# Graph network on one core: the equality one-hots of a group made by two wide VectorE instructions in place of six narrow ones

## The chip, the cores and the metric

The kernel runs on one core of a Trainium2 chip. The metric is the device time of one execution in microseconds (us). Before the change it is 1136.53 us, the median of 3 runs (1135.17 to 1138.17).

## The reference, cut to what matters

Two graph layers run over 3125 nodes with 128 features and 100000 edges, which are sorted by destination. The first layer takes, for each destination, the maximum over its edges of a message; the second takes means over the edges, twice.

```python
# layer 0
msgs = z[edge_dst] @ Wd + z[edge_src] @ Ws + edge_weight[:, None] * ww[None, :] + bm
agg = jax.ops.segment_max(msgs, edge_dst, num_segments=n)
x = layernorm(x + relu(z @ W1a + agg @ W1b + b1) @ W2 + b2)
# layer 1, twice: a mean over the edges' source rows, then dense layers
agg = jax.ops.segment_sum(x[src], dst, num_segments=n_nodes)
mean = agg / jnp.maximum(deg, 1.0)[:, None]
```

## The kernel before

The edges are worked off in 196 groups of 512 (the last has 160 real edges in one superbatch). A group has two superbatches of 256 edges, a superbatch two halves (`u`) of 128. A counter `k` steps through the groups; each engine has its own instruction order, written out by hand, and in step `k` the engines work on neighbouring groups. What matters here:

- **GpSimd** gathers the source rows of a group from memory by four indirect DMAs (`gathers`, L1037) of 128 rows each. The index of a row is read from `src_n` in SBUF. Seven groups of the 196 (`PICKED`: 17, 28, 37, 48, 60, 80, 93) aren't gathered, and five (`OWN`) take three gathers in place of four. The ring `gring` holds four groups: the gathers of group g wait until TensorE has transposed group g - 4 (`t_ps`).
- **TensorE** in step k adds the edge weights' part (L1614) and transposes the gathered rows (L1626) for group k; then, in `adjacent(k-2)`, it multiplies the one-hots of group k-2 into a count matrix (L1675, L1678) and picks the maxima of its segments (L1685), which raises `ae_ps` by one for each superbatch; `products(k-1)` transposes the scan's result (L1665). Between these stand tile work and pieces of the second layer (L1748, L1706), and for the picked groups products with other one-hots (L1785).
- **VectorE** in step k runs the scan of group k over 512 columns (`scan`, L1225, one operand of which lies in PSUM), `pick(k-1)` (L1217) and `one_hots(k-1)`, then tile work, and in the steps before a picked group makes that group's source one-hots (L1303).
- `one_hots(g)` makes, for each superbatch and half, `hot_l` (128 edges by 128 columns: which source row within its tile), `hot_d` (128 by 325) and, once a superbatch, `hot_x` (128 by 25). TensorE waits for `made` before it uses them. The buffers are rings of `HR` = 4 superbatches, so VectorE waits for `ae_ps` before it writes them again.
- After step 195 the second layer's rest follows: L1748, L1861, L1875 and L1910 on TensorE.

Of the kernel before, what the change touches and what calls it, by code (L numbers as in the profile page):

```python
# [4 lines left out]
P = 128  # L5
# [4 lines left out]
NT = -(-N // P)  # L10
LASTN = N - (NT - 1) * P
SB = 256
NS = -(-E // SB)
# [6 lines left out]
COLS = NT * W  # L20
AW = N + W
AWORDS = NT * AW // 2
HR = 4
# [109 lines left out]
def supers(g):  # L133
    return range(2 * g, min(2 * g + 2, NS))
# [6 lines left out]
def gnn_kernel(nc, x, src, dst, w, Wm, bm, W1, b1, W2, b2, W1lT, b1l, W1rT, W2lT, b2l, W2rT, out):  # L141
    f32, i32, bf16, f16, f32r = mybir.dt.float32, mybir.dt.int32, mybir.dt.bfloat16, mybir.dt.float16, mybir.dt.float32r
    ALU, ACT = mybir.AluOpType, mybir.ActivationFunctionType
# [17 lines left out]
    with ctx:  # L161
# [3 lines left out]
        def sem(name):  # L165
            return ctx.enter_context(nc.semaphore(name))
# [196 lines left out]
        made, picked, ae_ps, ae_sb = sem("made"), sem("picked"), sem("ae_ps"), sem("ae_sb")  # L363
# [738 lines left out]
        def _(dve):  # L1102
# [97 lines left out]

            def usual():
                def one_hots(g):
                    for s in supers(g):
                        if s >= HR:
                            dve.wait_ge(ae_ps, s - HR + 2)
                        r = s % HR
                        for u in range(2):
                            nc.vector.tensor_scalar(hot_l[:, r, u, :], i_key[:, 0:P], lo_n[:, u, s:s + 1], None, ALU.is_equal)  # L1208
                            nc.vector.tensor_scalar(hot_d[:, r, u, :], i_key[:, 0:COLS], key_n[:, u, s:s + 1], None, ALU.is_equal)  # L1209
                        nc.vector.tensor_scalar(hot_x[:, r, 0:NT], i_hi[:, 0:NT], key2_n[:, s:s + 1], None, ALU.is_equal).then_inc(made, 1)  # L1210

                def pick(g):
                    if g >= 2:
# [91 lines left out]
                for k in range(SLOTS):  # L1305
# [5 lines left out]
                    if slots(k, 1) is not None:  # L1311
                        pick(k - 1)
                        one_hots(k - 1)
# [682 lines left out]
```

## Time and profile before

| | |
|---|---|
| median of 3 runs | 1136.53 us |
| the profiled execution | 1136.4 us |
| its span, first to last instruction | 1134.6 us |
| PE busy | 997.1 us (88%) |
| VectorE (DVE) busy | 894.9 us (79%) |
| GpSimd (POOL) busy | 757.0 us (67%) |
| ScalarE (ACT) busy | 500.8 us (44%) |
| mean granted TensorE clock | 0.958 |

Busy shares are means over the whole program. GpSimd's "issue" is time in which the engine waited for nothing that the profile shows, between two of its instructions. The VectorE instructions overlap at their ends, so the recorded duration of one is longer than the step from its start to the next one's start.

### The profile page before, as it was taken

The numbers are of one execution on the slowest core, as the hardware profiler recorded it, in microseconds if no ns is written. First come the engines' busy times: TensorE is split into PE (matmuls) and PEld (weight loads), VectorE is DVE, ScalarE is ACT, GpSimd is POOL, SyncE is SP. The second block draws the span as 40 slices with busy tenths as digits, with TensorE's granted clock in tenths as the row PEclk, the third lists the DMA queues.
The fourth block names the chain that finished last, engine by engine and source line by source line (L and its number), as shares of the span: only waits on it lengthen the run. The fifth ranks groups of instructions, "written<-read, shape, count | busy, mean of one in ns | idle before, by whom it ended". The sixth has DMA issues, their size and how long they took to land.

```text
span 1134.6 us, 23462 instructions
## 1 busy us (share of the span) xinstructions
PE 997.1 (88%) x6407; PEld 735.8 (65%) x6449; DVE 894.9 (79%) x3127; ACT 500.8 (44%) x1434; POOL 757.0 (67%) x802
## 2 busy tenths in 40 slices
PE   4689999999997999978797879886889899899997
PEld 4367767767765777756665656565556577656776
DVE  6488999999886999897777778777788788746455
ACT  3256766666542656533333323333324233312664
POOL 6657777777777777777777777777777777200332
PEclk9789999999997999989898889999999999999999
DMA  8724344344344343334434334433344354446221
GB/s 210 214 61 94 92 98 109 94 99 114 89 97 106 91 119 97 91 85 127 110 87 93 90 97 129 105 91 89 87 132 110 106 150 97 117 134 177 83 58 42
DMA packets 123128, 121.14 MB, mean 107 GB/s; under 512 B 24307, under 2 KB 106392, under 8 KB 122989
## 3 DMA queue, kind: packets, MB, share of 16 engines
q1 hardware_dynamic: 95920, 69.21, 22.7%
q0 software_dynamic: 23968, 49.13, 18.0%
q10 hardware_dynamic: 3101, 1.21, 0.4%
q8 instruction: 54, 0.88, 0.3%
q14 instruction: 85, 0.70, 0.2%
HBM read 105.60 MB, written 13.88 MB: 105 GB/s over the span
## 4 chain that ended last, share of the span: by engine, by line
PE 36%; POOL 30%; issue 15%; DVE 12%; DMA 3%; SPq 2%; ACT 1%; ACTq 1%; DVEq 0%
POOL area L1037 30%; PE bank L1910 7%; PE bank L1748 5%; PE bank L1685 5%; PE bank L1675 3%; PE bank L1626 3%; PE bank L1785 3%; DVE area L1225 2%; DVE area L1209 2%; PE bank L1665 2%; PE bank L1875 2%; DVE area L1208 2%; PE bank L1614 2%; PE bank L1861 1%; PE bank L1706 1%
## 5 line engine op out<-in xcount | busy, mean ns | idle before, releaser
L1037 POOL DMA_INDIRECT area<-zs_d,area x729 | 705.4, 968 | 234.8 <-issue 219.3
L863 ACT CAST adj_w<-bank 128x325 f32 x391 | 176.2, 451 | 472.5 <-PE bank L1685 415.1
L1225 DVE TENSOR_TENSOR_SCAN area<-area,bank 128x512 f32<-128x512 bf16 x196 | 249.7, 1274 | 144.1 <-PE bank L1626 126.5
L1209 DVE TENSOR_SCALAR area<-area 128x325 bf16<-128x325 f16 x782 | 249.5, 319 | 0.0
L1685 PE MATMUL bank<-area 128*128 128x104 f32 x1564 | 234.0, 294 | 0.1
L1208 DVE TENSOR_SCALAR area<-area 128x128 bf16<-128x128 f16 x782 | 212.1, 271 | 0.0
L1685 PEld LDWEIGHTS bank<-area 128*128 128x128 f32 x1564 | 204.7, 204 | 11.3 <-ACT area L869 1.9
L1675 PE MATMUL bank<-area 128*128 128x325 bf16 x782 | 157.2, 316 | 22.0 <-DVE area L1210 15.8
L1626 PE MATMUL bank<-ident,area 128*128 128x128 f32 x734 | 123.1, 291 | 45.8 <-DMA area<-zs_d,area 45.4
L1626 PEld LDWEIGHTS bank<-ident,area 128*128 128x128 f32 x734 | 78.1, 142 | 91.1 <-DMA area<-zs_d,area 57.2
L1748 PE MATMUL bank<-adj_w,area 128*128 128x512 bf16 (+5 forms) x497 | 108.5, 357 | 24.6 <-DMA area<-parts_d 8.6
L1665 PE MATMUL bank<-ident,area 128*128 128x128 f32 x782 | 121.0, 278 | 0.0
L869 ACT COPY area<-bank 128x512 f32<-128x512 f32 x196 | 118.3, 604 | 4.7 <-issue 3.3
L909 ACT CAST hot_r<-adj_w 128x512 fp32r<-128x512 bf16 x175 | 98.0, 622 | 48.3 <-DVE adj_w L1303 47.5
L1058 POOL CAST counts<-adj_w 128x512 fp32r<-128x512 bf16 (+2 forms) x45 | 28.2, 631 | 124.1 <-DVE area L1357 74.7
L1785 PE MATMUL bank<-hot_r,zs_r 128*128 128x512 f32 (+1 forms) x350 | 99.7, 414 | 0.4 <-issue 0.3
L1210 DVE TENSOR_SCALAR area<-area 128x25 bf16<-128x25 bf16 x391 | 97.4, 249 | 0.0
L1665 PEld LDWEIGHTS bank<-ident,area 128*128 128x128 f32 x782 | 96.1, 151 | 0.3 <-issue 0.3
L1614 PE MATMUL bank<-area,ww 9*128 9x512 bf16 x189 | 74.4, 394 | 20.9 <-DMA area<-wp_d 20.8
L1675 PEld LDWEIGHTS bank<-area 128*128 128x128 bf16 x782 | 61.6, 100 | 45.9 <-DVE area L1210 22.9
L1748 PEld LDWEIGHTS bank<-adj_w,area 128*128 128x128 bf16 (+1 forms) x525 | 48.6, 98 | 64.3 <-issue 21.4
L1678 PE MATMUL bank<-area 128*128 128x25 bf16 x390 | 74.5, 191 | 0.0
(174 smaller groups left out, 1067.6 us busy)
## 6 DMA issues: line engine op xcount, KB each, us to landing
area<-mask_d SPq DMA_DIRECT2D x195, 128.0 KB
area<-zs_d,area POOLq DMA_INDIRECT x729
area<-zs_d SPq DMA_DIRECT2D x640, 0.5 KB
area<-parts_d SPq DMA_DIRECT2D x20, 384.0 KB, 7.6
area<-wp_d SPq DMA_DIRECT2D x195, 9.0 KB
zr_d<-area SPq DMA_DIRECT2D x24, 128.0 KB
area<-zr_d SPq DMA_DIRECT2D x6, 512.0 KB, 4.5
area<-scale_d SPq DMA_DIRECT2D x11, 256.0 KB, 4.3
```

Of the source, the lines that this page charges most:

```text
L863: nc.scalar.copy(adj[:, :, bass.ds(at, W)], A_BANK[s % 2][:, 0:COLS].rearrange("p (h w) -> p h w", w=W))
L869: nc.scalar.copy(St[:, 0:n], S_BANK[:, 0:n]).then_inc(st_sb, 1)
L1037: pool.indirect_dma_start(gring[:, g % GR * 4 + s % 2 * 2 + u, :], None, x if g < RAW else zs_d[0:N, :], bass.IndirectOffsetOnAxis(ap=firs ...
L1208: nc.vector.tensor_scalar(hot_l[:, r, u, :], i_key[:, 0:P], lo_n[:, u, s:s + 1], None, ALU.is_equal)
L1209: nc.vector.tensor_scalar(hot_d[:, r, u, :], i_key[:, 0:COLS], key_n[:, u, s:s + 1], None, ALU.is_equal)
L1225: nc.vector.tensor_tensor_scan(S[:, g % 2, 0:n], mask[:, g % MR, 0:n], (L_BANK if g in PICKED else T_BANK[g % 2])[:, 0:n], S[:, (g + 1) % ...
L1626: last = nc.tensor.matmul(o[:, b * P:(b + 1) * P], rows, ident[:, :], start=False, stop=b == n // P - 1, is_transpose=True)
L1665: last = nc.tensor.transpose(S_BANK[:, b * P:(b + 1) * P], S[:, g % 2, b * P:(b + 1) * P], ident[:, :])
L1675: last = nc.tensor.matmul(o[:, 0:COLS], hot_l[:, r, u, :], hot_d[:, r, u, :], start=u == 0, stop=u == 1 and s == 0)
L1685: last = nc.tensor.matmul(o[:, 384:384 + WIDE * W].rearrange("p (n w) -> p n w", w=W), St[:, b * P:(b + 1) * P], sel[:, g % 2, u, s % 2, : ...
L1748: last = nc.tensor.matmul(o[:, 0:b - a], row[0:k, i * F:(i + 1) * F], adj[0:k, h, a:b], start=start and i == 0, stop=stop and i == 2)
L1785: last = nc.tensor.matmul(L_BANK[:, :], part_of[0:n, h - SPLITS[at][1], :], hot_r[u % HOTS][0:n, :], start=h == 0 and part_of is zs_high[a ...
```

## The change

For a group, the four instructions that made `hot_l` (128 columns each, a compare of `i_key` with one number per partition) become one compare of two tensors on 512 columns: `i_key`, in fp16 and repeated over superbatch and half, against `lo_n`, in f32 and repeated over the columns. The two that made `hot_x` (25 columns each) become one compare of two tensors on 50 columns. The four of `hot_d` stay, now side by side. The group waits once for `ae_ps`, for the count that its second superbatch waited for before; `made` rises by two at the end in place of one at a time.

```diff
                 def one_hots(g):
-                    for s in supers(g):
-                        if s >= HR:
-                            dve.wait_ge(ae_ps, s - HR + 2)
-                        r = s % HR
+                    s, m = 2 * g, len(supers(g))
+                    r = s % HR
+                    if s >= HR:
+                        dve.wait_ge(ae_ps, min(s + m, NS) - HR + 1)
+                    low = lo_n[:, :, s:s + m].unsqueeze(3).broadcast_to([P, 2, m, P])
+                    count = i_key[:, 0:P].unsqueeze(1).unsqueeze(1).broadcast_to([P, 2, m, P])
+                    nc.vector.tensor_tensor(hot_l[:, r:r + m, :, :].rearrange("p s u e -> p u s e"), count, low, ALU.is_equal)
+                    for n in range(m):
                         for u in range(2):
-                            nc.vector.tensor_scalar(hot_l[:, r, u, :], i_key[:, 0:P], lo_n[:, u, s:s + 1], None, ALU.is_equal)
-                            nc.vector.tensor_scalar(hot_d[:, r, u, :], i_key[:, 0:COLS], key_n[:, u, s:s + 1], None, ALU.is_equal)
-                        nc.vector.tensor_scalar(hot_x[:, r, 0:NT], i_hi[:, 0:NT], key2_n[:, s:s + 1], None, ALU.is_equal).then_inc(made, 1)
+                            nc.vector.tensor_scalar(hot_d[:, r + n, u, :], i_key[:, 0:COLS], key_n[:, u, s + n:s + n + 1], None, ALU.is_equal)
+                    carried = key2_n[:, s:s + m].unsqueeze(2).broadcast_to([P, m, NT])
+                    tiles_at = i_hi[:, 0:NT].unsqueeze(1).broadcast_to([P, m, NT])
+                    nc.vector.tensor_tensor(hot_x[:, r:r + m, 0:NT], tiles_at, carried, ALU.is_equal).then_inc(made, m)
```

On VectorE one step of the loop stood like this before, from the scan (L1225) and the pick (L1217) to the next step's source one-hots (L1303); `area` is the tensor that all of these buffers are cut from:

```order
L1225 SCALAR_TENSOR_TENSOR area<-area,bank 128x512 [waits scanned,l_mask0,t_ps]
L1217 TENSOR_TENSOR area<-area 128x52 [waits ae_ps]
L1208 TENSOR_SCALAR area<-area 128x128 [waits ae_ps]
L1209 TENSOR_SCALAR area<-area 128x325
L1208 TENSOR_SCALAR area<-area 128x128
L1209 TENSOR_SCALAR area<-area 128x325
L1210 TENSOR_SCALAR area<-area 128x25
L1208 TENSOR_SCALAR area<-area 128x128 [waits ae_ps]
L1209 TENSOR_SCALAR area<-area 128x325
L1208 TENSOR_SCALAR area<-area 128x128
L1209 TENSOR_SCALAR area<-area 128x325
L1210 TENSOR_SCALAR area<-area 128x25
```

In the changed kernel the lines behind the edit have numbers that are 5 higher, and the same step of VectorE stands like this:

```order
L1230 SCALAR_TENSOR_TENSOR area<-area,bank 128x512 [waits scanned,l_mask0,t_ps]
L1222 TENSOR_TENSOR area<-area 128x52 [waits ae_ps]
L1209 TENSOR_TENSOR area<-area 128x2x2x128 [waits ae_ps]
L1212 TENSOR_SCALAR area<-area 128x325 x4
L1215 TENSOR_TENSOR area<-area 128x2x25
```

Ten instructions have become six. The 512-column compare has moved to the front, right behind the pick, and the second wait on `ae_ps` has moved ahead of the whole block. The instructions of the other engines stand as they did.

## Rows read from the trace of the kernel before

**Rows 1.** Busy time of the engines in three stretches, with clock and DMA
```profile
73.00:490.00 417.00, 391.19 (x2609) 292.81 (x2618) 378.57 (x1396) 245.41 (x686) 318.33 (x324) 0.98 0.40 99
...
805.00:973.00 168.00, 151.05 (x1055) 106.38 (x1066) 139.67 (x469) 54.52 (x187) 127.47 (x134) 0.98 0.44 115
973.00:1135.00 162.00, 151.60 (x767) 112.72 (x768) 89.87 (x276) 70.54 (x152) 28.26 (x46) 0.98 0.36 101
```

**Rows 2.** GpSimd's waits from 73 to 973 us: total, times, longest
```profile
POOL area L1037 <- issue: 211.5, 694, 0.3
```

**Rows 3.** The gathers by line, 73 to 490 and 490 to 973 us
```profile
L1037 POOL DMA_INDIRECT area<-zs_d,area x324 | 319.2, 985 | 98.7 <-issue 95.7 <-PE bank L1626 3.1
...
L1037 POOL DMA_INDIRECT area<-zs_d,area x384 | 366.3, 954 | 117.1 <-issue 115.8 <-PE bank L1626 1.2
```

**Rows 4.** Timeline: last gather and scan of groups 161 and 195
```profile
805.01 0.95 POOL L1037 DMA_INDIRECT area<-zs_d,area  x1 [0.31 <-issue]
...
809.52 1.28 DVE L1225 TENSOR_TENSOR_SCAN area<-area,bank 128x512 f32<-128x512 bf16 x1 [2.08 <-PE bank L1626]
...
972.14 0.95 POOL L1037 DMA_INDIRECT area<-zs_d,area  x1 [0.30 <-issue]
...
980.80 0.74 DVE L1225 TENSOR_TENSOR_SCAN area<-area,bank 128x256 f32<-128x256 bf16 x1
```

**Rows 5.** VectorE groups by shape: busy us, mean ns
```profile
L1208 DVE TENSOR_SCALAR area<-area 128x128 bf16<-128x128 f16 x782 | 212.1, 271 | 0.0
...
L1210 DVE TENSOR_SCALAR area<-area 128x25 bf16<-128x25 bf16 x391 | 97.4, 249 | 0.0
...
L1347 DVE TENSOR_TENSOR area<-area 128x512 f32<-128x512 f32 x6 | 4.2, 692 | 0.2
```

**Rows 6.** Timeline: a pick, the block of one-hots, what follows
```profile
977.85 0.20 DVE L1217 TENSOR_TENSOR area<-area 128x52 f32<-128x52 bf16 x1
977.97 0.25 DVE L1208 TENSOR_SCALAR area<-area 128x128 bf16<-128x128 f16 x1
...
979.24 0.25 DVE L1208 TENSOR_SCALAR area<-area 128x128 bf16<-128x128 f16 x1
979.40 0.30 DVE L1209 TENSOR_SCALAR area<-area 128x325 bf16<-128x325 f16 x1
979.62 0.23 DVE L1210 TENSOR_SCALAR area<-area 128x25 bf16<-128x25 bf16 x1
979.75 0.22 DVE L1284 CAST area<-area 128x128 bf16<-128x128 f32 x1
```

**Rows 7.** Timeline: gathers that start under long VectorE instructions
```profile
12.54 1.22 DVE L1134 TENSOR_TENSOR adj_w<-adj_w 128x1020 f32<-128x1020 f32 x1 [2.59 <-ACT adj_w L805]
12.88 1.70 POOL L1037 DMA_INDIRECT area<-in_x_dram,first_n  x1 [0.30 <-issue]
...
21.02 1.20 DVE L1164 TENSOR_TENSOR adj_w<-adj_w 128x1024 f32<-128x1024 f32 x1
...
21.61 1.43 POOL L1037 DMA_INDIRECT area<-in_x_dram,area  x1 [0.30 <-issue]
...
39.24 1.22 DVE L1225 TENSOR_TENSOR_SCAN area<-area,bank 128x512 f32<-128x512 bf16 x1 [4.98 <-issue]
39.31 0.94 POOL L1037 DMA_INDIRECT area<-zs_d,area  x1 [0.30 <-issue]
```

**Rows 8.** Timeline: first and last gather counted under a new compare
```profile
83.11 0.25 DVE L1208 TENSOR_SCALAR area<-area 128x128 bf16<-128x128 f16 x1
...
83.46 0.94 POOL L1037 DMA_INDIRECT area<-zs_d,area  x1 [0.31 <-issue]
...
964.16 0.25 DVE L1208 TENSOR_SCALAR area<-area 128x128 bf16<-128x128 f16 x1
...
964.49 0.94 POOL L1037 DMA_INDIRECT area<-zs_d,area  x1 [0.30 <-issue]
```

**Rows 9.** TensorE's waits for the one-hots: total, times, longest
```profile
PE bank L1675 <- DVE area L1210: 15.8, 19, 2.7
```

## The prediction

> **What bounds the kernel now.** I first read the busy time by stretches [rows 1]. From 73 to 490 us TensorE is busy 391 of 417 us and VectorE 379, and from 805 to 973 they have 151 and 140 of 168: three engines run side by side at high load, and a share of the span doesn't say which one sets the pace. GpSimd looks the least loaded (318 of 417). So I next read what GpSimd waits for. Between 73 and 973 us, 694 of its pauses have nothing that releases them, 211.5 us in all, none longer than 0.3 us [rows 2]. The gathers stand in an unbroken row: 0.94 us for one, 0.30 of issue behind it, 1.25 us from start to start. With 708 of them in that stretch [rows 3] this is 885 of the 900 us, and the rest is gathers that took longer than 0.94. The ring of four groups never stops them. **GpSimd's chain of gathers is therefore the bound from 73 to 973 us**, and what lengthens or shortens a gather moves its end one for one.
>
> Two more stretches belong to the end time. The first is the start up to 72 us. The other runs from the last gather to the end, where TensorE is busy 152 of 162 us [rows 1]: TensorE alone. Between them lies a small reserve. In group 161 the scan starts 3.6 us after its last gather ends (805.01 + 0.95 to 809.52), and TensorE had been waiting for that landing. In group 195 it starts 7.7 us after (973.09 to 980.80) [rows 4]. At the end, the consumers are some 4 us behind where the gathers would let them be.
>
> **The change on VectorE.** In a block of today the 128-column compare takes 0.16 us from its start to the next start, the 325-column one 0.22, the 25-column one 0.13; the block takes 1.78 us (977.97 to 979.75) [rows 6]. The recorded 271 and 249 ns [rows 5] overlap, so multiplying those would double the gain. Removed are 4 x 0.16 + 2 x 0.13 = 0.90 us. No row shows a 512-column compare of an fp16 with an f32 tensor; the nearest is L1347, two f32 tensors of 512 columns in SBUF, 692 ns [rows 5], of which some 0.08 overlap the next: 0.61 us. From below it could be like the 25-column compare of one tensor (0.13), from above 0.69. I take 0.61, since one input here is f32 too. The 50-column one is like the pick on 52 columns, 0.12 us from start to start (977.85 to 977.97) [rows 6]. Added: 0.73. VectorE gains 0.17 us a group, 33 us of work over 196 groups. After 73 us this is worth nothing by itself, since VectorE isn't the bound; the cover is GpSimd's chain. Before 72 us five groups pass and the gathers do wait for TensorE: about -1 us.
>
> **The moved wait.** The whole block now waits for the first superbatch's L1685 of the group before; earlier half of it ran ahead. Where that wait binds, the block ends up to 0.89 - 0.17 = 0.7 us later. Behind it on VectorE stand tile work and the next scan; TensorE's L1675 of the next step waits for it, which it does 19 times now for 15.8 us [rows 9]. From below the cost is 0, from above 19 x 0.7 = 13 us of TensorE's waiting, and that counts only where TensorE has used up its distance to the gathers. I take 0; the reserve below covers a few us.
>
> **The change on GpSimd.** This is where I look for the time. At 12.54 us VectorE starts a compare of two SBUF tensors, which lasts until 13.76. A gather that starts at 12.88 takes 1.70 us and ends at 14.58, 0.82 after the compare's end. The one at 21.02 ends at 22.22, and the gather from 21.61 ends at 23.04: again 0.82 later [rows 7]. A free gather takes 0.94. So about 0.12 us after its start a gather needs something that a VectorE instruction with two SBUF inputs holds, and it waits for that instruction's end. A gather under the scan, which reads one operand from PSUM, isn't held: 0.94 us at 39.31 [rows 7]. The 128-column compares of today hold it little: in 490 to 973 us, where hardly any other one-hots are made, the mean gather is 954 ns against 944 free, 10 ns each [rows 3], or 7 us over 708 gathers for all ten instructions of a block. Six of ten go: -4 us.
>
> The new compare holds it for long. I count its hold from 0.07 us after its start (it starts under the pick's end) to 0.69. A read hits that with chance 0.62 / 1.25 = 0.50 and then waits 0.31 us in the mean: 0.154 us a group, 29 us over the 190 blocks after 72 us. Because the phases may not be random, I also laid the compare at the place of each block's first L1208 in the trace and took every gather whose start plus 0.125 falls within: 88 gathers, 27.3 us together. The first is the gather at 83.46 under the block from 83.11, the last that at 964.49 under 964.16 [rows 8]. I take 27. From below it is 0 if no read falls in, from above 0.69 x 0.69 / 2.5 x 190 = 36 us.
>
> [...]
>
> **The sum.** Gathers +27 (the new compare) and -4 (the old ones), start -1, and 3 of the 4 us of reserve, since the consumers catch up while the gathers run slower. The result is +19, made against the profiled execution's own 1136.4 us, which is the median within 0.1 us: **1155.5 us**.
>
> **Rivals.**
> [...]
> - *The compare runs at twice the rate* (0.05), as fp16 against bf16 might: 0.41 us, hold 0.34, 0.34 x 0.34 / 2.5 x 190 = 9 us: 1140 us. Against it: `lo_n` is f32.
> - *Nothing is held* (0.10): the two-tensor compare with repeated operands leaves the gathers alone, and the freed 128-column compares give 4 us back, the start 1: 1131 us, the other side. It decides if the new holding is below 5 us, that is under 26 ns a group. For it: neither of the held gathers lies under a compare with an fp16 input or repeated operands. Against it: the hold itself, twice to 0.01 us [rows 7].
> - *Full holding and the late wait* (0.06): 36 us from random reads on the whole 0.69, nothing given back, and TensorE pays part of the moved wait where it works off its backlog: 1172 us or more.
> - The forecast itself has 0.69, with its own range of 1146 to 1168.
>
> **How the numbers follow.** A measurement here tells 0.3%, 3.4 us, from no change. Slower: the forecast 0.69, the full holding 0.06, half of the first rival 0.05 and 0.02 of the second: 0.82. Within: 0.05 and 0.03, 0.08. Faster: 0.10. The range goes from 1139 (the first rival's time) to 1170; outside are the faster case, the lowest part of the first rival and most of the highest.
>
> **What would show it.** The mean of L1037 rises from 985 and 954 ns in the two stretches by some 30 ns each, with far more gathers above 1.0 us; each held one ends 0.82 us after the end of the compare at L1209. The row of gathers still has no wait of its own after 73 us and ends near 995 rather than 973. L1209 shows x196 near 690 ns, L1215 near 190; VectorE's busy time falls by some 30 to 60 us. The stretch behind the last gather keeps its 162 us within 3. I am wrong if the gathers keep their 985 and 954 ns, or if the compare takes much less than 0.6 us, or if GpSimd begins to wait for TensorE.

## The result

The changed kernel takes 1147.79 us (median of 9 runs, 1141.48 to 1150.76), the kernel before 1137.52 us (9 runs, 1135.17 to 1144.4). The ratio, taken between the means of the runs, is 1.0077, with a 95% interval of 1.0051 to 1.0103: **slower by 8.8 us, where 19 were forecast** (the medians lie 10.3 apart). The profiled execution took 1144.2 us, 7.8 more than that of before.

The gathers of the changed kernel by line, 73 to 490 us and 490 to 984 us (count, busy us, mean ns, idle before), to be read beside [rows 3]:

```profile
L1037 POOL DMA_INDIRECT area<-zs_d,area x323 | 320.6, 992 | 98.9 <-issue 96.0 <-PE bank L1631 2.9
...
L1037 POOL DMA_INDIRECT area<-zs_d,area x387 | 377.3, 975 | 118.0 <-issue 117.4 <-PE bank L1631 0.6
```

The mean rose from 985 to 992 ns in the first stretch and from 954 to 975 in the second. GpSimd's pauses are still nearly all without a releaser, beside [rows 2]:

```profile
POOL area L1037 <- issue: 213.1, 699, 0.3
```

The end of the chain in the timeline of the changed kernel, the last two gathers and the last scan, to be read beside [rows 4]:

```profile
981.72 1.16 POOL L1037 DMA_INDIRECT area<-zs_d,area  x1 [0.30 <-issue]
983.18 0.94 POOL L1037 DMA_INDIRECT area<-zs_d,area  x1 [0.30 <-issue]
...
989.09 0.74 DVE L1230 TENSOR_TENSOR_SCAN area<-area,bank 128x256 f32<-128x256 bf16 x1
```

The last gather ends at 984.1 us in place of 973.1: 11 us later. The last scan follows 5.0 us after it and no longer 7.7, so some 3 us of the reserve are used. From the last scan to the end of the span it takes 153.2 us (153.8 before).

VectorE by shape (count, busy us, mean ns), beside [rows 5]:

```profile
L1230 DVE TENSOR_TENSOR_SCAN area<-area,bank 128x512 f32<-128x512 bf16 x195 | 249.2, 1278 | 188.0 <-PE bank L1631 166.3 <-PE bank L1622 10.0 <-issue 7.2
L1212 DVE TENSOR_SCALAR area<-area 128x325 bf16<-128x325 f16 x782 | 190.1, 307 | 0.0
L1209 DVE TENSOR_TENSOR area<-area 128x512 bf16<-128x512 f16 x195 | 133.9, 687 | 11.6 <-PE bank L1690 11.3
...
L1215 DVE TENSOR_TENSOR area<-area 128x50 bf16<-128x50 bf16 x195 | 38.7, 198 | 0.0
```

The wide compare takes 687 ns. VectorE's busy time fell from 894.9 to 846.6 us, and what it saved turned into waiting: the scan now sits idle for TensorE's transposes for 166.3 us, and those wait for gathers. Two held gathers in the timeline of the changed kernel:

```profile
539.86 0.69 DVE L1209 TENSOR_TENSOR area<-area 128x512 bf16<-128x512 f16 x1
539.87 1.50 POOL L1037 DMA_INDIRECT area<-zs_d,area  x1 [0.30 <-issue]
...
655.01 0.68 DVE L1209 TENSOR_TENSOR area<-area 128x512 bf16<-128x512 f16 x1
655.04 1.47 POOL L1037 DMA_INDIRECT area<-zs_d,area  x1 [0.30 <-issue]
```

Both gathers end 0.82 us after the compare does (541.37 to 540.55, 656.51 to 655.69), as in [rows 7]. So do 74 of the 75 gathers after 73 us that start more than 0.02 us after the compare and 0.15 us or more before its end; the last of the 75 stays out 0.16 us longer. The 325-column compare that comes next has started by then, some 0.08 us before.

A gather that starts ahead of the compare, mostly under the pick, isn't held by it, though it is still running when the compare begins:

```profile
294.18 0.95 POOL L1037 DMA_INDIRECT area<-zs_d,area  x1 [0.30 <-issue]
294.21 0.69 DVE L1209 TENSOR_TENSOR area<-area 128x512 bf16<-128x512 f16 x1
```

21 gathers start in the 0.12 us up to the compare's start: 15 take the 0.94 us of a free gather, five up to 0.05 us more, and one stays out beyond the compare. The traces of e9 and e5 show the same: of their 20 and 17 such gathers none takes 0.05 us more.

**Where the 11 us are.** I call the hold of a gather its time above 944 ns, and put it down to the VectorE instruction that runs 0.124 us after the gather's start (0.944 less the 0.82 that a held gather still takes). I call that instant its read. Added over all gathers that start after 73 us, one profile for each kernel:

| kernel | under the wide compare | under the source one-hots | under all others | in all | last gather ends |
|---|---|---|---|---|---|
| before | - | 6.2 | 10.6 | 16.8 | 973.1 |
| changed | 21.4 (103 gathers) | 1.5 | 4.0 | 26.9 | 984.1 |

So the wide compare adds 21 us, and 11 are given back elsewhere. Of the 103 gathers, 84 are held by 0.015 us or more; of the other 19, 18 started ahead of the compare or within 0.02 us of its start, and one has its read at the very end.

### The profile page after: what moved, and what is told of

Same layout as the page of the kernel before. It is cut to its first block, busy times and chain, and to the rows that moved or that the text cites. A ratio compares the mean times of both kernels' runs of the same rounds, so it can differ in the third digit from the quotient of the medians.

```text
span 1142.3 us, 22681 instructions
## 1 busy us (share of the span) xinstructions
PE 1002.0 (88%) x6407; PEld 740.8 (65%) x6449; DVE 846.6 (74%) x2346; ACT 501.7 (44%) x1434; POOL 768.8 (67%) x802
## 4 chain that ended last, share of the span: by engine, by line
POOL 48%; PE 23%; issue 17%; DVE 5%; DMA 5%; SPq 2%; ACTq 0%; ACT 0%; DVEq 0%
POOL area L1037 48%; PE bank L1915 7%; PE bank L1753 3%; PE bank L1690 2%; DMA area<-zs_d,area 2%; PE bank L1880 2%; PE bank L1631 2%; PE bank L1680 1%; PE bank L1670 1%; PE bank L1866 1%; DMA area<-wp_d 1%; PE bank L1790 1%; DVE area L1254 1%; DVE area L1230 1%; DMA area<-parts_d 1%
## 5 line engine op out<-in xcount | busy, mean ns | idle before, releaser
L1037 POOL DMA_INDIRECT area<-zs_d,area x729 | 717.1, 984 | 234.0 <-issue 221.3
L1230 DVE TENSOR_TENSOR_SCAN area<-area,bank 128x512 f32<-128x512 bf16 x196 | 250.0, 1275 | 188.0 <-PE bank L1631 166.3
L1212 DVE TENSOR_SCALAR area<-area 128x325 bf16<-128x325 f16 x782 | 190.1, 307 | 0.0
L1631 PE MATMUL bank<-ident,area 128*128 128x128 f32 x734 | 127.0, 298 | 64.2 <-DMA area<-zs_d,area 64.2
L1631 PEld LDWEIGHTS bank<-ident,area 128*128 128x128 f32 x734 | 80.9, 146 | 111.7 <-DMA area<-zs_d,area 81.4
L1209 DVE TENSOR_TENSOR area<-area 128x512 bf16<-128x512 f16 x196 | 134.4, 685 | 11.6 <-PE bank L1690 11.3
L1753 PE MATMUL bank<-adj_w,area 128*128 128x512 bf16 (+5 forms) x497 | 109.1, 358 | 21.5 <-DMA area<-parts_d 7.3
L1670 PE MATMUL bank<-ident,area 128*128 128x128 f32 x782 | 121.0, 278 | 0.8 <-DVE area L1230 0.8
L1670 PEld LDWEIGHTS bank<-ident,area 128*128 128x128 f32 x782 | 95.7, 150 | 1.0 <-DVE area L1230 1.0
L1619 PEld LDWEIGHTS bank<-area,ww 9*128 9x128 bf16 x189 | 17.2, 91 | 87.9 <-issue 64.7
```

The source lines that it names most:

```text
L1037: pool.indirect_dma_start(gring[:, g % GR * 4 + s % 2 * 2 + u, :], None, x if g < RAW else zs_d[0:N, :], bass.IndirectOffsetOnAxis(ap=firs ...
L1209: nc.vector.tensor_tensor(hot_l[:, r:r + m, :, :].rearrange("p s u e -> p u s e"), count, low, ALU.is_equal)
L1212: nc.vector.tensor_scalar(hot_d[:, r + n, u, :], i_key[:, 0:COLS], key_n[:, u, s + n:s + n + 1], None, ALU.is_equal)
L1230: nc.vector.tensor_tensor_scan(S[:, g % 2, 0:n], mask[:, g % MR, 0:n], (L_BANK if g in PICKED else T_BANK[g % 2])[:, 0:n], S[:, (g + 1) % ...
L1631: last = nc.tensor.matmul(o[:, b * P:(b + 1) * P], rows, ident[:, :], start=False, stop=b == n // P - 1, is_transpose=True)
L1670: last = nc.tensor.transpose(S_BANK[:, b * P:(b + 1) * P], S[:, g % 2, b * P:(b + 1) * P], ident[:, :])
```

## The experiments

A ratio is to runs of the kernel before that were taken beside it; its median was 1137.75 us beside e1 to e4, 1136.82 beside e5 to e8, 1137.62 beside e9 to e11 and 1137.32 beside e12. "Holds" are counted as above, each from one profile.

**e1: the wide compare without its second SBUF operand.**

```diff
-                    count = i_key[:, 0:P].unsqueeze(1).unsqueeze(1).broadcast_to([P, 2, m, P])
+                    count = T_BANK[(g + 1) % 2][:, 0:2 * m * P].rearrange("p (u s e) -> p u s e", s=m, e=P)
```

> The changed kernel, but the 512-column compare takes its first operand from a PSUM bank (bank 0 or 1, which stands idle there) in place of the counts in SBUF; the values compared are therefore not the counts, and the output is not the reference's. Columns, instructions and waits stay those of the changed kernel. Theory (a compare of two SBUF tensors holds a gather's read of its indices): no gather ends 0.82 us after this compare any more; the holds under it fall from some 21 us to under 2, the last gather ends between 960 and 968 us where it was 984 in the changed kernel and 973 before, and the time is 1130 to 1137 us, under the kernel before's or level with it. Rival (the moved wait, or the wide instruction's own length, makes TensorE late): the time stays at the changed kernel's 1144 to 1150, and the last gather ends near 984.

Measured: 1128.36 us against 1137.75, ratio 0.9909 (0.9890 to 0.9928): faster than the kernel before. The time is a little under the range given. 116 gathers have their read under the wide compare, and their holds are 0.5 us together, where they were 21.4; the last gather ends at 964.2. 82 of them start more than 0.02 us after it, as the held ones of the changed kernel do, and none of them but one (0.07 us) is held by more than 0.01. The compare is as long as in the changed kernel (683 ns), so it isn't VectorE's time that costs. Such a gather in e1's timeline:

```profile
86.18 0.68 DVE L1209 TENSOR_TENSOR area<-bank,area 128x512 bf16<-128x512 f32 x1
86.45 0.94 POOL L1037 DMA_INDIRECT area<-zs_d,area  x1 [0.30 <-issue]
```

**e2: the wide compare twice.**

```diff
+                    link(nc.vector.tensor_tensor(hot_l[:, r:r + m, :, :].rearrange("p s u e -> p u s e"), count, low, ALU.is_equal))
                     nc.vector.tensor_tensor(hot_l[:, r:r + m, :, :].rearrange("p s u e -> p u s e"), count, low, ALU.is_equal)
```

> The changed kernel with the 512-column compare done twice, the second behind the first. Theory (holding): the holds under it double from some 21 us to 38 to 48, the last gather ends near 1000 to 1010 where it was 984, and the time rises to 1158 to 1172 us. Rival (VectorE's work or the moved wait costs the time): 0.7 us more of VectorE a group over 195 groups; where VectorE sets the step, in the first third, it could cost 10 to 20 us, but the gathers keep their mean of 984 ns.

Measured: 1172.47 us, ratio 1.0318 (1.0298 to 1.0337), at the top of the range given. 210 gathers are caught, holds 43.5 us, the last gather ends at 1004.5. The gathers' line on the page (all 729):

```profile
L1037 POOL DMA_INDIRECT area<-zs_d,area x729 | 736.3, 1010 | 234.9 <-issue 219.8 <-PE bank L1632 14.6 <-PE bank L1611 0.6
```

With none, one and two wide compares on SBUF the holds under them are 0.5, 21 and 44 us, and the last gather ends at 964, 984 and 1004. That, with e8 below, settles the mechanism and its price.

**e3: the narrow compares left out.**

```diff
+                            if s < HR:
-                            nc.vector.tensor_scalar(hot_l[:, r, u, :], i_key[:, 0:P], lo_n[:, u, s:s + 1], None, ALU.is_equal)
+                                nc.vector.tensor_scalar(hot_l[:, r, u, :], i_key[:, 0:P], lo_n[:, u, s:s + 1], None, ALU.is_equal)
```

> The kernel before, with the four 128-column compares of a group left out from the third group on (the first four superbatches' are made, and their contents stay in the buffers; the output is not the reference's). It measures what taking the narrow compares away gives back to the gathers. The prediction put it at 4 us for six of ten instructions; the trace of the changed kernel looks like 11. If 4 is right, the last gather ends at 969 to 971 us where it was 973; if 11 is right and comes from the narrow compares, 961 to 965. If the fall of the holds under the bursts of source one-hots (6.2 us to 1.4) was a matter of phase, it can come out at either. Time 1127 to 1136 us.

Measured: 1121.62 us, ratio 0.9856 (0.9842 to 0.9870), last gather at 960.5: both below the ranges given. The holds after 73 us fall from 16.8 to 4.7: 2.2 under source one-hots, 2.5 under others.

```profile
L1037 POOL DMA_INDIRECT area<-zs_d,area x729 | 694.5, 953 | 232.8 <-issue 221.5 <-PE bank L1627 10.1 <-PE bank L1606 1.1
```

So the four narrow compares cost the gathers 12 us, where my estimate was 4 for six instructions. 16.8 - 12.1 + 21.4 = 26.1, where 26.9 were counted in the changed kernel. The 21.4 are themselves from the changed kernel; e1, which takes them away, has 9.1 us of holds left, 8.6 of them outside the wide compare, where the changed kernel has 5.5. The terms fit to some 3 us and not better.

**e4: the wait alone.**

```diff
-                    for s in supers(g):
-                        if s >= HR:
-                            dve.wait_ge(ae_ps, s - HR + 2)
+                    if 2 * g >= HR:
+                        dve.wait_ge(ae_ps, supers(g)[-1] - HR + 2)
+                    for s in supers(g):
```

> The kernel before, with only the wait moved: the whole block of a group waits for the count that its second superbatch waited for. Theory (the wait costs nothing, GpSimd's chain sets the pace): within 0.3% of before, 1134 to 1140 us, the last gather at 971 to 976. Rival (the moved wait is what costs the changed kernel's 9 us): 1143 to 1148 us.

Measured: 1135.54 us, ratio 0.9988 (0.9972 to 1.0004), last gather at 972.8. The wait costs nothing that these runs can tell.

**e5 and e6: each half of the change alone.** In e5 the two narrow compares of `hot_x` come back behind the four of `hot_d`; in e6 the block is that of before with this in place of its two narrow ones (in part; `carried` and `tiles_at` as in the change):

```diff
-                        nc.vector.tensor_scalar(hot_x[:, r, 0:NT], i_hi[:, 0:NT], key2_n[:, s:s + 1], None, ALU.is_equal).then_inc(made, 1)
+                    nc.vector.tensor_tensor(hot_x[:, r:r + m, 0:NT], tiles_at, carried, ALU.is_equal).then_inc(made, m)
```

> Only the first half of the change: the 512-column compare for hot_l (and its moved wait), while the two 25-column compares of hot_x stay as before. Theory (the 512-column compare's hold is the cost): nearly the whole change, 1142 to 1150 us, 19 to 24 us of holds under it, the last gather at 982 to 987. Rival (the 50-column compare of two tensors adds a good part): below 1142 us.

> Only the second half of the change: the 50-column compare for hot_x, with the four 128-column compares as before. Theory: it holds a gather for at most 0.12 us and seldom; one instruction fewer. 1133 to 1139 us, the last gather at 970 to 975. Rival (the wide hot_x costs a part of the 9 us): 1140 us and more.

Measured: e5 1152.77 us, ratio 1.0150 (1.0123 to 1.0177), above the range I gave; e6 1132.78 us against 1136.82, ratio 0.9962 (0.9950 to 0.9974), just under it. The last gathers end at 989.8 and 968.6, outside the ranges too. The halves pull against each other. The wide `hot_l` alone costs 1.5%, and the wide `hot_x` gives back 0.4% alone and 0.7% beside the other half. In e5 the holds are 17.5 us under the wide compare, 5.8 under source one-hots and 8.8 under others; in e6 they are 1.2 and 11.2 (6.2 and 10.6 before). So what the wide `hot_x` gives back alone lies where source one-hots follow the block; beside the wide `hot_l` (e5 against the changed kernel) it is 4.3 us there and 4.8 elsewhere.

**e7: the narrow compares read from PSUM.**

```diff
-                            nc.vector.tensor_scalar(hot_l[:, r, u, :], i_key[:, 0:P], lo_n[:, u, s:s + 1], None, ALU.is_equal)
+                            nc.vector.tensor_scalar(hot_l[:, r, u, :], T_BANK[(g + 1) % 2][:, 0:P], lo_n[:, u, s:s + 1], None, ALU.is_equal)
```

> The kernel before, all ten instructions kept, but the four 128-column compares of a group read their columns from an idle PSUM bank in place of SBUF; the values compared are not the counts, and the output is not the reference's. Leaving these compares out took 12 us off the gathers' holds. Theory (each of them holds a gather because both its tensors lie in SBUF, and in a row of instructions the gather isn't let in between): the holds fall as much as when they are left out, from 17 us after 73 us to 5 to 7, the last gather at 961 to 965, the time 1123 to 1131 us. Rival (a gather is let in only where VectorE pauses, whatever it reads; ten instructions in a row hold it longer than six): holds stay at 14 to 17 us, the last gather at 970 to 974, the time 1133 to 1139 us.

Measured: 1148.22 us, ratio 1.0094 (1.0073 to 1.0114), against both forecasts. The theory's half on the holds came out: they fall to 4.4 us with all ten instructions kept. But from PSUM, where its columns are f32, one narrow compare takes 340 ns in place of the 271 of f16 columns in SBUF, VectorE fell behind, and the gathers were stopped by the ring. Lines of the lists of waits over the whole program (who, for whom, us, times, longest), e7's and then, for the second, that of before; the first is to be read beside [rows 9]:

```profile
PE bank L1675 <- DVE area L1210: 38.8, 49, 3.0
POOL area L1037 <- PE bank L1626: 37.2, 24, 8.5
...
POOL area L1037 <- PE bank L1626: 14.6, 16, 8.6
```

After 73 us the gathers' pauses behind L1626 are 28.8 us in all, the longest 4.2, where before they were 4.3 us, none longer than the 0.3 of an issue. So VectorE isn't far from being the bound, in the kernel before too: from its start to the next start a narrow compare takes 0.26 us from PSUM and 0.16 from SBUF, and four times 0.1 us a group was enough to cross it. The profiled execution of e7 took 1155.39 us.

**e8: the counts laid into PSUM, with the right result.** Ahead of the pick VectorE copies the counts into the bank that its scan has just finished with, and the wide compare reads them there:

```diff
+                def lay_counts(g):
+                    dve.wait_ge(scanned, min(g + 2, NG))
+                    linked[0] += 1
+                    nc.vector.tensor_copy(T_BANK[(g + 1) % 2][:, 0:P], i_key[:, 0:P]).then_inc(order, 1)
...
+                    dve.wait_ge(order, linked[0])
+                    count = T_BANK[(g + 1) % 2][:, 0:P].unsqueeze(1).unsqueeze(1).broadcast_to([P, 2, m, P])
```

> The changed kernel made free of the hold, with its right result: before each group's pick VectorE copies the 128 counts into the PSUM bank whose scan it has just finished, and the 512-column compare reads them from there. It adds a copy of 128 columns, some 0.16 us a group, and a wait for the scan. Theory: no hold under the wide compare; the added copy is covered by the gathers after 73 us. The last gather at 962 to 968 us, the time 1127 to 1134 us, faster than both kernels. Rival (the copy from SBUF holds gathers as the narrow compares did, or VectorE becomes the bound in the first third): 1135 us and more.

Measured: 1136.80 us (12 runs, 1126.87 to 1143.10), ratio 0.9991 (0.9965 to 1.0016): the rival's time. No gather is held under the wide compare (0.0 us over 106), and the last one ends at 964.0, as forecast; but five pauses of the gathers last over 0.5 us, 5.1 us together, the last scan comes 12 us after the last gather (8 in e1), and the runs scatter more than those of any other kernel here. The profiled one took 1131.90 us. Here the compare reads the counts repeated over superbatch and half, as in the changed kernel, so it isn't the repetition that holds. That the added copy (293 ns, 196 times) takes up the room that e1 had is likely, but not shown.

**e9: two-byte operands throughout.**

```diff
-             (i32, 2, NS), (f32, 2, NS), (f32, 2, NS), (bf16, 2, 2 * NG), (bf16, NS + 1),
+             (i32, 2, NS), (f16, 2, NS), (f32, 2, NS), (bf16, 2, 2 * NG), (bf16, NS + 1),
```

> The changed kernel with lo_n kept in fp16 in place of f32 (its numbers are 0 to 127), so that all three tensors of the 512-column compare are of two bytes; the result stays right. Theory A (the compare then runs at twice the rate): some 0.41 us for one, and the holds, which grow with the square of its length, fall from 21 us to 5 to 9; the last gather at 968 to 974, 1130 to 1138 us. Theory B (a repeated operand keeps it at the single rate): it stays at 680 to 690 ns, and all stays as in the changed kernel, 1142 to 1150 us.

Measured: 1149.97 us, ratio 1.0105 (1.0074 to 1.0136). Theory B's time: the compare keeps its length, and the holds under it are 23.1 us. Whether the repeated operand is what keeps it there, no run shows. VectorE's row by shape:

```profile
L1209 DVE TENSOR_TENSOR area<-area 128x512 bf16<-128x512 f16 x195 | 134.1, 688 | 15.1 <-PE bank L1690 14.9
```

Since nothing else differs, this is also a second profile of the changed kernel: the holds elsewhere are 5.5 us in both.

**e10: two compares of 256 columns.**

```diff
-                    nc.vector.tensor_tensor(hot_l[:, r:r + m, :, :].rearrange("p s u e -> p u s e"), count, low, ALU.is_equal)
+                    count = i_key[:, 0:P].unsqueeze(1).broadcast_to([P, 2, P])
                     for n in range(m):
+                        low = lo_n[:, :, s + n:s + n + 1].broadcast_to([P, 2, P])
+                        nc.vector.tensor_tensor(hot_l[:, r + n, :, :], count, low, ALU.is_equal)
```

> The changed kernel with the 512-column compare split in two of 256 columns, the first in front of the first superbatch's two 325-column compares and the second in front of the second's. If the hold lasts for one instruction and a waiting gather gets in at its end, two holds of 0.35 us cost half of one of 0.69: 21 us of holds become 8 to 12, the last gather at 970 to 977, 1133 to 1141 us. Rival (the holds follow the columns in all): 1143 us and more.

Measured: 1146.98 us, ratio 1.0077 (1.0050 to 1.0104); the holds after 73 us are 30 us in all. That is the rival's time. I had expected 8 to 12 us of holds under the two compares. 80 gathers that start under one of them (more than 0.02 us behind its start) have 14.0 us, and each is let in at the compare's end, though the next compare has started. The rest comes from gathers that start ahead. At the first compare, which stands behind the pick, 2 of 27 such gathers are held to its end; at the second, which stands behind two 325-column compares, it is 21 of 23, and four more whose read falls under the 325-column compare itself: 8.7 us. One of these four, in e10's timeline:

```profile
423.34 0.51 DVE L1212 TENSOR_SCALAR area<-area 128x325 bf16<-128x325 f16 x2
423.62 1.39 POOL L1037 DMA_INDIRECT area<-zs_d,area  x1 [0.30 <-issue]
423.77 0.41 DVE L1210 TENSOR_TENSOR area<-area 128x256 bf16<-128x256 f16 x1
```

The gather's read at 423.74 falls under a 325-column compare, isn't let in at its end, and waits out the 256-column one behind it as well: it ends at 425.01, 0.83 us after the latter's end (424.18). So a hold can be handed on, here from a 325-column compare to the wide one behind it. In the other order it isn't, as the 80 show. The longest case of e10 is a gather of 2.88 us that starts at 79.40 and stays out over nine instructions, until the last source one-hot ends.

**e11: an instruction between the block and the source one-hots.** The kernel before, with

```diff
-                        nc.vector.tensor_scalar(hot_x[:, r, 0:NT], i_hi[:, 0:NT], key2_n[:, s:s + 1], None, ALU.is_equal).then_inc(made, 1)
+                        last = nc.vector.tensor_scalar(hot_x[:, r, 0:NT], i_hi[:, 0:NT], key2_n[:, s:s + 1], None, ALU.is_equal)
+                        if s == supers(g)[-1]:
+                            last = nc.vector.tensor_tensor(hot_x[:, r, NT:NT + 1], i_hi[:, 0:1], i_hi[:, 1:2], ALU.is_equal)
+                        last.then_inc(made, 1)
```

> The kernel before with one instruction added at the end of each block of one-hots: a compare of two tensors on a single column, some 0.06 us, into a padding column that nobody reads; the result stays right. It stands between the block and the source one-hots that follow it in the steps ahead of a picked group. Theory (a gather that meets a row of overlapping one-tensor compares stays out until the row ends, and an instruction of another kind in between lets it in; this is what the wide hot_x does for the gathers beside saving a little of VectorE): the holds under source one-hots fall from 6 us to 1 to 2, the last gather at 967 to 970, 1131 to 1135 us, as with the wide hot_x alone. Rival (it is the shorter block of VectorE, or the missing narrow compares, that helps there): 1136 to 1139 us, the last gather at 972 to 975.

Measured: 1133.67 us against 1137.62, ratio 0.9967 (0.9949 to 0.9984). One more instruction makes the kernel faster. The holds under source one-hots fall from 6.2 to 3.1 us, not to 1 or 2, and the others from 10.6 to 9.4; the last gather ends at 968.1. What the instruction takes away are the long holds: one gather stays out beyond the instruction under which its read falls, where 13 did before (0.5 us and 6.8). The holds that end with that instruction grew from 9.9 to 11.8 us.

**e12: e6 with such an instruction between the superbatches.**

```diff
+                        if s == 2 * g:
+                            nc.vector.tensor_tensor(hot_x[:, r, NT:NT + 1], i_hi[:, 0:1], i_hi[:, 1:2], ALU.is_equal)
```

> The wide hot_x of e6, with the narrow 128-column compares, and a compare of two tensors on one padding column between the two superbatches of a group, so that no more than four narrow compares stand in a row; the result stays right. Theory (shorter rows hold gathers less): the holds outside the source one-hots fall from 11 us to 6 or 7, the last gather at 963 to 967 us, 1128 to 1132 us. Rival (only the instruction that happens to run at the read matters, and the small compare holds gathers itself): 1131 to 1136 us, the last gather at 967 to 971, no better than the wide hot_x alone.

Measured: 1136.64 us, ratio 0.9987 (0.9967 to 1.0008), last gather at 973.6: no better than e6, as the rival had it, and slower than the rival's range. The holds outside the source one-hots rose from e6's 11.2 to 14.4 us. An inserted two-tensor compare is no sure way to let a gather in.

## Why the prediction went in the right direction with the wrong size

**The bound was right.** GpSimd's chain of gathers stands unbroken from 73 us on in both kernels, and what lengthens a gather moves its end. e2 and e3 move the time by 35 and 16 us by adding or leaving out work of VectorE, which itself has time to spare there.

**The hold was right.** It lasts until the compare's end, and is gone when one operand lies in PSUM (e1, e8). That the gather reads its indices 0.12 us after its start is the simplest reading of this; no run separates that read from other work of the gather. The size was forecast as 27 us from 88 gathers and measured as 21.4. Both counts took in gathers that aren't held: those that start ahead of the compare or with it. I had let the hold begin for reads 0.07 us after the compare's start, and in the changed kernel it begins at about 0.14, which is a gather that starts just behind the compare. Laid over the trace of before again with 0.14, my count gives 77 gathers and 21.5 us. So most of what this term had too much comes from there.

**The step that failed is "Six of ten go: -4 us".** The term was mis-sized: the changed kernel has 11.3 us less of holds outside the wide compare, and e3 measures 12.1 for the four 128-column compares alone. I took the price of the narrow instructions from 490 to 973 us, 10 ns a gather, and left the 41 ns of the first stretch [rows 3] to the source one-hots made there. But of that stretch's 13.1 us only 6.2 lie under source one-hots; the gathers under all else were held by 25 ns each, not 10. And the source one-hots' own holds change with the block ahead of them: they are 6.2 us before and 7.2 in e4, 2.2 in e3, 1.5 in the changed kernel and 1.2 in e6, but 5.8 in e5. Nor do holds go in proportion to the instructions: from 490 us on they are 3.7 us before and 0.7 in e3, so four of ten instructions carry four fifths.

The traces tell two kinds of hold apart, of 0.015 us or more: those that end with the instruction under which the read falls, and those that go on over one or more further instructions.

| kernel | end with it: gathers, us | go on: gathers, us |
|---|---|---|
| before | 131, 9.9 | 13, 6.8 |
| e4 | 132, 10.0 | 10, 5.8 |
| e5 | 160, 23.2 | 14, 9.0 |
| changed | 155, 25.7 | 2, 1.1 |
| e6 | 154, 11.3 | 1, 0.6 |
| e3 | 55, 3.9 | 2, 0.8 |

Half of the 11 us given back are the second kind, which is rare and dear. In seven of its 13 cases before, the read falls under a source one-hot and the hold goes on over those behind it; why the block ahead bears on that, no run shows. It nearly goes where the narrow `hot_x` are replaced (changed, e6) and where the 128-column compares are left out (e3). In e5, which keeps the narrow `hot_x`, it stays: 9.0 us against the changed kernel's 1.1, where all its holds together are 5.2 us more.

With the two measured terms, 21 and -11 in place of 27 and -4, the sum is +10 on the last gather, where 11 were measured, and with 3 us of reserve +7 on the time, where the profiled executions differ by 7.8.

**The small terms.** The start gained nothing (the tenth gathered group starts at 64.8 us, 64.4 before; I had -1). The reserve gave 3 us, as forecast. The moved wait costs nothing (e4). VectorE's gain is worth nothing by itself here; e7 shows how close its limit is.

**The rivals.** That nothing is held is refuted: 75 of 75 gathers that started under the compare were held. The double rate didn't occur: the compare took 687 ns, and 688 with two-byte operands throughout (e9). A compare of two-byte columns with one number per partition takes 357 ns for 512 columns in the trace of before (L1303), where the two f32 tensors of L1347 take 692; no run shows a compare of two tensors of that width in 0.41 us. The compare didn't fall between reads either: 103 fell under it. The range's lower end of 1139 us, with 0.10 of chance, stood for that case, and it took the compare to follow its group's last gather at a fixed distance where the landing sets the step. No run shows such a distance. In the trace of before, TensorE's transposes wait 0.1 us or more for the landing in 31 groups after 73 us, and the first compare behind the scan starts 3.5 to 6.0 us after the last gather ends; in the changed kernel there are 50 such groups, with 3.5 to 6.4 us. Reads are 1.25 us apart, so both spreads take in every place between two of them.

**What stays open:** after which instructions a held gather is let in. Overlap alone doesn't decide it: the 325-column compare that overlaps the end of the wide one kept out 1 gather of 75, while the second two-tensor compare of e10 kept out 25 that had started ahead of it, under a 325-column one. e12 runs against a simple rule of rows: its holds that go on are few (6 gathers, 1.9 us), and the others grew (13.5 us, in e6 11.3). Besides, the holds outside the wide compare differ by some 3 us between kernels that should be alike there (8.6 us in e1, 5.5 in the changed kernel and in e9).

**A version that beats both:** the wide `hot_x` with the narrow `hot_l` (e6), 0.4% under the kernel before. e11 has the same gain within its interval.

## What to carry to other kernels

When GpSimd issues gathers one after the other, it can be the bound at 67% busy, as here: look for pauses that nothing releases, and multiply the time from start to start by the number of gathers. Then price each VectorE instruction by what it does to a gather and not only by its own length: here a 687 ns one with two SBUF inputs cost 21.4 us of holds over the program, one PSUM operand brought them to 0.5 (e1), 20 of 21 gathers that started first escaped it within 0.05 us, and four narrow compares a group, in a row of overlapping ones, cost 12 us as well (e3). Take the price of a thing that you remove from each stretch where it stands, or leave it out in a run and measure.

## What the hardware showed that I had not expected

- A compare of two SBUF tensors holds a gather that starts behind its own start, to its end, and, where the pick stands ahead of it, hardly one that started before it (changed kernel: 75 of 75 held, and of the 21 others only one for more than 0.05 us).
- A gather held by a VectorE instruction is sometimes kept out by the next ones too (e10: 1.39 us and 2.88 us for gathers of 0.94; 13 gathers with 6.8 us before). Behind the wide compare it is let in, though the next has started (74 of 75).
- A one-tensor compare on 128 columns takes 340 ns with its columns in PSUM as f32 (e7) and 271 with them in SBUF as f16 (before).
- A compare of two tensors, all of two bytes and both repeated over columns or groups, takes 688 ns on 512 columns, the same as with an f32 operand (e9).
- An added instruction of 166 ns a group made the kernel 0.3% faster (e11).
